# Layer 2 attention: the query projection ahead of the third scores, and no whole copy of the turned queries

## What is computed

```python
xn = layernorm(x, g1); q = xn @ Wq.T; k, v = split(xn @ Wkv.T, 64)   # 16 query heads, 1 key/value head
q = l2norm(q.reshape(b, n, 16, 64).transpose(0, 2, 1, 3) * 16) * 4
k = l2norm(k) * 4
sim = where(causal, einsum('bhid,bjd->bhij', q, k), -max)
out = einsum('bhij,bjd->bhid', softmax(sim), v)
out = layernorm(out.reshape(b, n, 1024) @ Wout.T, g2)
x = x + out + (silu(xf @ wg.T) * (xf @ wu.T)) @ wd.T                 # xf = layernorm(x), hidden 384
```

## Time and profile before

| what | value |
|---|---|
| median of 3 runs | 1247.28 us (1245.82 to 1248.21) |
| profiled execution | 1250.76 us, its span 1249.0 us |
| mean granted TensorE clock | 0.975 |
| PE busy (matmuls) | 1155.6 us, 93% |
| PEld busy (weight loads) | 788.6 us, 63% |
| DVE busy (VectorE) | 875.2 us, 70% |
| ACT busy (ScalarE) | 668.0 us, 53% |
| POOL busy (GpSimd) | 486.9 us, 39% |

### The profile page before, as it was taken

The page is one execution under the profiler, slowest core; times in us unless marked ns, Lnnn a source line. Parts: engine busy times, 40 slices in busy tenths (PEclk is TensorE's granted clock), DMA queues, the critical chain, the costliest instruction groups (busy, mean ns, idle before and its releaser), DMA issues.

```text
span 1249.0 us, 26722 instructions
## 1 busy us (share of the span) xinstructions
PE 1155.6 (93%) x8667; PEld 788.6 (63%) x8667; DVE 875.2 (70%) x2425; ACT 668.0 (53%) x1290; POOL 486.9 (39%) x691
## 2 busy tenths in 40 slices
PE   5999999999999999898599999999999999999896
PEld 3656665665666654798366757657576576765764
DVE  7888888888888895564465757657576575764744
ACT  2666676667676655454362553725527255273550
POOL 5222212121222311564373461734717347273350
PEclk8999999999999997899699999999999999999999
DMA  3311202020101000122011030110301203012030
GB/s 92 99 44 45 57 26 56 26 73 18 27 18 27 19 18 1 47 67 53 9 35 27 13 55 8 30 29 13 55 1 31 36 13 55 0 29 38 9 52 9
DMA packets 43717, 42.31 MB, mean 34 GB/s; under 512 B 7040, under 2 KB 36224, under 8 KB 43648
## 3 DMA queue, kind: packets, MB, share of 16 engines
q0 software_dynamic: 11008, 17.31, 8.0%
q1 hardware_dynamic: 32640, 24.15, 7.1%
HBM read 13.72 MB, written 6.75 MB: 16 GB/s over the span
## 4 chain that ended last, share of the span: by engine, by line
issue 18%; PE 13%; POOL 8%; ACT 5%; DMA 4%; DVE 3%; POOLq 0%; ACTq 0%; DVEq 0%
PE gather L496 6%; DMA arena<-arena 4%; PE ring_a L496 3%; POOL arena L1284 3%; ACT arena L1508 3%; POOL arena L1205 2%; PE pair L496 2%; POOL q_len L1246 1%; DVE q_parts L1992 1%; POOL late L1284 1%; ACT arena L1488 1%; ACT q_parts L1496 1%; POOL arena L1267 1%; DVE stats L1547 0%; PE ring_a L500 0%
## 5 line engine op out<-in xcount | busy, mean ns | idle before, releaser
L1351 ACT ACTIVATE arena<-ring_a 128x384 f32<-128x384 f32 (+1 forms) x512 | 253.4, 550 | 151.3 <-PE ring_a L496 151.1
L1100 POOL TENSOR_SCALAR_AFFINE_SELECT arena<-arena 128x512 f32<-128x512 f32 x128 | 83.2, 650 | 369.5 <-ACT arena L1351 369.3
L496 PE MATMUL ring_a<-q_max,rows 128*128 128x384 f32 (+1 forms) x512 | 198.2, 391 | 2.0 <-DVE q_max L1657 1.8
L1643 DVE CUSTOM_DVE_ANT_0 arena<-pair,arena 128x384 bf16<-128x384 f32 (+1 forms) x269 | 161.2, 614 | 23.8 <-PE pair L496 19.8
L1508 ACT ACTIVATE arena<-ring_a 128x1024 f32<-128x1024 f32 x96 | 98.8, 1029 | 108.0 <-PE ring_a L496 108.0
L1246 POOL TENSOR_TENSOR q_len<-q_sum,exponents 128x8 f32<-128x8 f32 x64 | 105.5, 1649 | 98.2 <-DVE q_sum L1973 97.9
L496 PE MATMUL ring_a<-q_parts,k_rows 64*128 64x384 f32 (+2 forms) x1152 | 125.7, 341 | 14.8 <-DVE q_parts L1992 13.8
L496 PE MATMUL ring_a<-arena,v_aug 128*32 128x384 f32 (+1 forms) x1024 | 125.6, 562 | 1.7 <-POOL arena L1100 0.6
L496 PE MATMUL pair<-arena,v_aug 128*64 128x512 f32 (+3 forms) x768 | 114.0, 439 | 4.1 <-ACT arena L1508 3.5
L496 PEld LDWEIGHTS ring_a<-q_parts,k_rows 64*128 64x128 f32 x1152 | 93.0, 187 | 33.3 <-DVE q_parts L1992 15.2
L496 PE MATMUL pair<-rows,q_rows 128*128 128x384 f32 (+1 forms) x269 | 110.1, 411 | 3.2 <-DMA rows<-k_rows 2.4
(11 more groups left out here) (274 smaller groups left out, 2318.7 us busy)
## 6 DMA issues: line engine op xcount, KB each, us to landing
arena<-arena POOLq DMA_DIRECT2D x32, 384.0 KB, 4.4
rows<-k_rows SPq DMA_DIRECT2D x128, 64.0 KB, 2.0
arena<-in_w SPq DMA_DIRECT2D x16, 256.0 KB, 2.8
slots_y<-arena SPq DMA_DIRECT2D x39, 64.0 KB, 1.7
x_all<-in_x SPq DMA_DIRECT2D x8, 256.0 KB, 3.6
tokens_x<-xn SPq DMA_DIRECT2D x8, 256.0 KB, 2.5
out<-o_t SPq DMA_DIRECT2D x8, 256.0 KB, 2.3
arena<-tokens_x,tokens_now POOLq DMA_INDIRECT x40, 2.8
```

Of the source, the lines that this page charges most:

```text
L496: return pe.matmul(out, lhs, rhs, start=start, stop=stop, skip_group_check=True)
L1100: pool.affine_select(out=v, in_=v, compare_op=ALU.is_ge, fill=0.0, base=0, pattern=[[0, HG], [1 if late else -1, P]], channel_multiplier=- ...
L1351: act.activation(probs[:, t % NT, h, 0:many], A.slot(("cols", c))[:, 0:many], ACT.Exp).then_inc(A.free.sem, A.free.add(1))
L1643: dve.tensor_tensor_reduce(dump[:, h % 2, 0:many], M.slot(("max", n))[:, 0:many], masks[:, m, at:at + many], 1.0, LOWEST, ALU.add, ALU.max ...
```

## The change

On TensorE, project_q(n + 2) moves from behind scores(n) to between the second and the third group of scores. On ScalarE, squares(n + 2) moves from behind the third exponential to between the second and the third. The whole copy `q_full` is dropped: `q_low` reads the turned query from its PSUM bank, and the waits that guarded `q_full` go with it. For the first query of a batch the release of ring R now follows `q_low`.

```diff
@@ TensorE, scores(n)
                     side_by_side([bank[:, 0:256] for bank in (S.slot(("probs", n, 1)), banks_d[1])], 2, n).then_inc(S.full.sem, S.full.add(1))
+                    if n + 2 < NP:
+                        project_q(n + 2)
                     pe.wait_ge(W.free.sem, W.fillable(b, ("probs", n, 2)))
...
                 for n in range(NP):
                     scores(n)
-                    if n + 2 < NP:
-                        project_q(n + 2)
                     if n + 1 < NP:
                         turn_q(n + 1)
@@ ScalarE, move_first_q
                 act.wait_ge(s["r_full"].sem, s["R"].filled(b, "q.T"))
-                act.wait_ge(SC["q_lo"].sem, SC["q_lo"].at(b, 0))
-                act.activation(q_full, s["R"].slot("q.T"), ACT.Copy)
                 act.activation(q_hi[:, 0, :], s["R"].slot("q.T"), ACT.Copy).then_inc(s["moved"].sem, s["moved"].add(1))
@@ ScalarE, attend
                 def q_turned(n):
                     act.wait_ge(S.full.sem, S.filled(b, ("q.T", n)))
-                    act.wait_ge(s["q_lo"].sem, s["q_lo"].at(b, n))
-                    sl = S.slot(("q.T", n))[:]
-                    act.activation(q_full, sl, ACT.Copy)
-                    act.activation(q_hi[:, n % QB, :], sl, ACT.Copy).then_inc(S.free.sem, S.free.add(1))
+                    act.activation(q_hi[:, n % QB, :], S.slot(("q.T", n))[:], ACT.Copy).then_inc(S.free.sem, S.free.add(1))
...
-                    for third in range(3):
-                        exp_of(n, third)
+                    exp_of(n, 0)
+                    exp_of(n, 1)
                     if n + 2 < NP:
                         squares(n + 2)
+                    exp_of(n, 2)
@@ VectorE
-            def q_low(n):
+            def q_low(n, turned):
 
                 s = SC
-                dve.tensor_tensor(q_lo[:, n % QB, :], q_full, q_hi[:, n % QB, :].bitcast(F32),
+                dve.tensor_tensor(q_lo[:, n % QB, :], turned, q_hi[:, n % QB, :].bitcast(F32),
                                   ALU.subtract).then_inc(s["q_lo"].sem, s["q_lo"].add(1))
@@ VectorE, first_q_turned
                 dve.wait_ge(R.free.sem, R.emptied(b, "k.T"))
+                q_low(0, R.slot("q.T"))
+                dve.wait_ge(SC["q_lo"].sem, SC["q_lo"].at(b, 1))
                 dve.sem_inc(R.free.sem, R.free.add(1))
-                q_low(0)
@@ VectorE, attend
                         dve.wait_ge(S.free.sem, S.emptied(b, ("q.T", n + 1)))
-                        q_low(n + 1)
+                        q_low(n + 1, S.slot(("q.T", n + 1))[:])
```

More of the change, by code:

```diff
@@ L370, in two_layers @@
         q_sq = arena[:, 14336:14848].rearrange("p (g d) -> p g d", d=D1)
-        q_full = arena[:, 14848:15360]
         q_nat = [t.rearrange("p (g d) -> p g d", d=D1) for t in
```

## The result

The changed kernel takes 1279.89 us (median of 4 runs, 1276.23 to 1282.66); the kernel before, on the same chip, 1246.55 (4 runs). The ratio is 1.0263, 95% interval 1.0233 to 1.0294: 33.3 us slower, where 32.3 were forecast. A repetition on another chip gave 1.0254 (1.022 to 1.0288).

The account below looks back on a forecast made before the run. TensorE was taken to set the pace, with the scaling just in time for the projection. Terms 0 + 0.94 + 2.73 + 0.37 = 4.04 us a batch, x 8 = 32.3, set against the 1247.28 median: 1279.5 us, range 1262 to 1290.

Parts of the forecast that it names:

- plain pair: Heads' pairs 2, 3 and 4 of a batch: projection waits for scaling until S + 2.12; 5.95 becomes 6.86 us, +0.91.
- pair 0: First pair of heads in a batch: projection starts unwaited, copy's 0.48 is eaten; between -0.18 and +0.05, taken as 0.
- pair 1: Second pair of heads: gate and up sit behind the delayed third exponential, values behind them; 7.97 for 7.03 us, +0.94.
- pairs 2 to 4: Three pairs of heads with one pattern: third scores wait behind the projection, 3 x 0.91 = +2.73 us a batch.
- pair 5: Pair with the last projection: +0.91 us, less the 0.54 wait for a folding transfer that goes; +0.37.
- TensorE's bound and the just-in-time scaling: Attention stage, layer 2: TensorE sets the pace; query scaling ends at S + 2.05, just before the projection at 2.12.
- Whole copy: ScalarE's copy, 0.48 us for 7 pairs: counts only where TensorE waits for the low half, pair 0 to 1.
- Rival 2: Projection doesn't wait, scaling through before S + 1.49; plain pairs stay 5.94, 3.8 us saved, 1243.5 us; chance 0.10.
- Low half from PSUM: VectorE's 64 subtractions read one operand from PSUM instead of SBUF: cost 0, 691 ns against 0.69 us.
- second drain: Upper bound: another array drain of 0.28 us where third scores follow the projection, giving +1.19 a pair.
- not 3: Rival: saved copy pays for the stall, 0.48 us back per pair against 0.91 lost; about 1248 us; chance 0.05.
- not 4: Rival: granted clock falls from 2.4 GHz level to 1.2 for one pair a batch; 47 us more, 1327; chance 0.04.

Follow-up runs that it names:

- copy-out on ScalarE: Changed kernel with the attention values copied out by ScalarE instead of VectorE: ratio 1.0046 on a slower chip, 1260.77 us and ratio 1.012 on another.
- the copy alone: Kernel before with only the whole copy dropped, old order kept: 1262.64 us against 1265.47, ratio 0.9975; repeated on another chip, ratio 1.0011.

## Why the prediction was right

The time was forecast to 0.4 us and the difference to 1.0, and the mechanism is shown, not only argued. That it came so close is in part luck, as the plain pair shows. Point by point, in us a batch:

| term | forecast | measured in the changed kernel | shown by |
|---|---|---|---|
| pair 0 | 0 | 5.80 - 5.88 = -0.08 | its own timeline |
| pair 1 | +0.94 | 8.02 - 7.03 = +0.99 | new order in two rounds only: the same +0.99 |
| pairs 2 to 4 | 3 x 0.91 | 3 x 0.93 | copy-out on ScalarE: 0.58 of each goes, 0.35 stays with the place |
| pair 5 | +0.37 | 8.52 - 8.05 = +0.47 | fold's wait gone in the timeline |
| sum | 4.04 | 4.2 | 82.80 - 78.62 |

*TensorE's bound and the just-in-time scaling*: right. The 0.37 that the view called a wait for the scaling was issue, as the comparison with pair 0 had it; in pair 2 of the old order the scaling earlier by a microsecond gave nothing, and an addition of 0.34 ahead of it cost 0.29. The prediction also had GpSimd's power 0.16 ahead of the length, and that is all the room there was: with the copy-out gone the power takes its place.

*Whole copy*: right in the sum: the order alone, with the copy, takes 0.48 more in pair 0. Rival 2 priced it wrongly. It gave the 0.48 behind pair 0 a value of 3.8 us; the copy alone showed that in the old order most of it is given back in pair 1, where the projection waits for a scaling that the copy doesn't advance.

*Low half from PSUM*: cost 0, as the row said: 692 ns for 693. The 62 extra cycles that the Trainium skill (VectorE: DVE Perf Modes, section on the TRN2 errata) gives such an operand aren't there for a subtraction of 512 fp32 columns.

*The plain pair*: 6.86 forecast, 6.87 measured, but that is closer than its parts. The projection started at 1.99, not 2.12, because the length took 0.16 us instead of the 0.27 of the earlier trace rows. From projection to third scores it was 1.09, not the 0.88 read from projection to turn. Third scores to turn was 0.89, not 0.91, and turn to values 0.59, not 0.64. The differences -0.13, +0.21, -0.02 and -0.05 cancel, and that they do is luck. The second of them belongs to the doubt about a second drain in the upper bound, and it is real. The sum put the cost of the place at nothing and gave all 0.91 to the uncovered wait; the copy-out on ScalarE shows 0.58 for the wait and 0.35 for the place.

*Pair 5*: mechanism right. Against the batch of the earlier trace rows, from which the forecast was made, it is 8.51 - 8.13 = 0.38 for 0.37; in most other batches the wait for the fold was shorter, and it is 0.47.

*Rivals*: the projection waits (not 2); the saved copy gives back 0.08 in a plain pair of the new order and nothing in the old, not 0.48 (not 3); the granted clock is 1.00 in every window of the batch (not 4).

## What to carry to other kernels

Before an instruction is moved earlier, ask when its inputs are ready, not only where its consumers wait: here the third scores were exactly the cover of the chain that the projection waits for. A wait that the profile puts down to a producer can be plain issue time; the same instruction at a place where the producer is long done tells which, and how much slack there is. When one chain is taken away, look for the next that ends at the same moment. And where a saved operation shortens one round, look in the next round for the wait that takes it back.

## What the hardware showed that was not expected

*One kernel on two chips.* On the chip of the first call the kernel before took 1265.47 us where others take 1244 to 1248. In the kernel without the copy one small operation of VectorE, the length, took 1.33 to 1.35 us once in each of seven of the eight batches; in the same kernel on another chip its longest was 0.37. VectorE's row and GpSimd's masks beside it:

```profile
724.52 1.34 DVE L1926 TENSOR_SCALAR q_len<-q_len 128x8 f32<-128x8 f32 x1
```

```profile
724.34 1.49 POOL L1283 TENSOR_SCALAR_AFFINE_SELECT arena<-arena 128x256 f32<-128x256 f32 x4
```

The masks are four instructions, 0.36 apart, each 0.40 long. A length that starts 0.05 to 0.33 behind the first of them takes 0.38 down to 0.16 and ends 0.42 to 0.49 behind its start, just after the first mask's end, on every chip; the long ones end 1.51 to 1.53 behind it, just after the fourth (724.52 + 1.34 = 725.86, 724.34 + 1.49 = 725.83). The Trainium skill (SBUF — State Buffer, section "Who interferes with whom") says of the SBUF port pair that VectorE and GpSimd share that the instruction which comes first has it to its end and the other is blocked, for VectorE instructions in a two-port mode or with two inputs in SBUF. The ends of the short ones agree with that rule; that this operation is in such a mode is shown by no run here, and by the rule a long one, which starts 0.18 behind the first mask, would wait for one mask and not for four. The 0.27 of the earlier trace rows is a short one behind a mask. In the changed kernel's plain pairs the length starts only when the fourth mask is about to end, and takes 0.16.

The long ones, in pair 4, aren't the first thing to differ. In pair 2 on the slower chip the square starts 1.73 to 1.81 us behind the projection's loads in those seven batches, with ScalarE idle ahead of it, where it is 1.30 to 1.32 on the other chip. GpSimd's power is late by that, the length of pair 3 waits for it, and pair 3 is 0.4 longer:

```profile
715.37 0.60 ACT L1477 ACTIVATE arena<-ring_d 128x512 f32<-128x512 f32 x1 [0.36 <-PE ring_d L495]
...
718.48 0.38 DVE L1926 TENSOR_SCALAR q_len<-q_len 128x8 f32<-128x8 f32 x1 [0.26 <-POOL q_len L1245]
```

The last batch, which fetches nothing for a next one, has neither the late square nor a long length. Why only this chip does so stays open, and the kernel before wasn't profiled there. The changed kernel with the copy-out on ScalarE was not touched by it in this stage (6.29 and 80.6 us on both chips), so that its ratio taken there, 1.0046, came out well below the 1.012 of the other chip. The 10 us that it still took more there lie ahead of the stage, which began at 624.2 instead of 610.0.

*Where groups on 64 rows and groups on 128 rows meet, time seems to be lost.* With nothing to wait for, the projection starts 0.20 later behind the second scores than the third scores did, and the third scores 0.21 later behind the projection than the turn did; a plain pair with both is 0.35 longer. The idle time ahead of the loads doesn't measure this: the projection of pair 0 starts 0.14 behind the last load of the second scores (778.33), the turn 0.36 behind that of the third scores (801.58), and the values 0.35 behind that of gate and up (788.43), where both groups use 128 rows. That the change of rows is the reason wasn't tried by itself.
